# Sixteen heads at a time: the maximum and subtraction of attention in one piece, score banks released together

## What is computed

```python
Q = _apply_rope(jnp.einsum('bsd,ed->bse', x, wq), cos, sin)
K = _apply_rope(jnp.einsum('bsd,ed->bse', x, wk), cos, sin)
V = jnp.einsum('bsd,ed->bse', x, wv)
# 16 heads of 16
scores = jnp.einsum('bhqd,bhkd->bhqk', Q, K) / math.sqrt(DIM_K)
weights = jax.nn.softmax(scores, axis=-1)
out = jnp.einsum('bhqk,bhkd->bhqd', weights, V)
```

## Time and profile before

| | us |
|---|---|
| median of three runs | 1210.27 |
| profiled execution | 1208.59 |
| span of the instructions in that execution | 1206.8 |
| PE busy, all stages | 977.0 (81%) |
| DVE busy | 692.0 (57%) |
| POOL busy | 650.4 (54%) |
| ACT busy | 524.6 (43%) |
| first scores matmul of attention | starts at 126.06 |
| last weighted values | start at 273.55 |

### The profile page before, as it was taken

How to read it: one execution, slowest core, us unless ns; L and a number is a source line. 1 busy time by engine, 2 the same in 40 slices (tenths; PEclk the granted TensorE clock), 3 DMA queues, 4 the chain that set the end, 5 groups by cost and what they waited for, 6 DMA issues and landing times. The chain is left out here.

```text
span 1206.8 us, 22495 instructions
## 1 busy us (share of the span) xinstructions
PE 977.0 (81%) x6878; PEld 869.3 (72%) x6878; DVE 692.0 (57%) x1539; ACT 524.6 (43%) x1080; POOL 650.4 (54%) x588
## 2 busy tenths in 40 slices
PE   6269699997569999398888699995169999999970
PEld 5258377776568898266666499995169999999970
DVE  1435599985666767569999346642723333333335
ACT  0011377772222222334433456563056676666650
POOL 0115578764544444223334489873057777777750
PEclk9689899997679999778888799996579999999995
DMA  7651345540000000000000510004346666666656
GB/s 255 194 219 49 85 153 160 167 139 18 0 1 1 0 0 0 0 1 0 0 0 0 212 75 14 14 27 166 139 147 203 197 194 198 193 202 190 205 177 225
DMA packets 61189, 127.32 MB, mean 106 GB/s; under 512 B 11929, under 2 KB 25954, under 8 KB 59794
## 3 DMA queue, kind: packets, MB, share of 16 engines
q1 hardware_dynamic: 52146, 103.81, 26.6%
q0 software_dynamic: 4848, 14.72, 3.5%
q10 hardware_dynamic: 4144, 8.16, 1.9%
HBM read 104.57 MB, written 24.31 MB: 107 GB/s over the span
## 5 line engine op out<-in xcount | busy, mean ns | idle before, releaser
L121 DVE CAST place<-place 128x512 fp32r<-128x512 f32 (+6 forms) x263 | 134.6, 544 | 212.9 <-PE moe_down L127 78.5
L2015 POOL TENSOR_TENSOR place<-place,place 128x512 fp32r<-128x512 f32 x84 | 138.0, 1643 | 51.5 <-DVE place L121 45.4
L2041 PE MATMUL moe_up<-place,place 128*128 128x128 f32 x1376 | 161.8, 276 | 0.0
L2041 PEld LDWEIGHTS moe_up<-place,place 128*128 128x128 f32 x1376 | 158.3, 193 | 0.0
L127 PE MATMUL moe_down<-place,place 128*128 128x256 f32 x1008 | 131.1, 286 | 0.4 <-POOL place L2015 0.4
L127 PEld LDWEIGHTS moe_down<-place,place 128*128 128x128 f32 x1008 | 123.4, 191 | 0.6 <-issue 0.6
L2113 ACT ACTIVATE place<-moe_up,place 128x128 f32<-128x128 f32 x344 | 97.5, 366 | 13.4 <-POOL place L2015 13.1
L2100 ACT ACTIVATE place<-place 128x2048 f32 x44 | 84.0, 1912 | 43.6 <-PEq L1837 29.9
L1168 POOL TENSOR_TENSOR place<-place,place 128x384 fp32r<-128x384 f32 x57 | 58.4, 1024 | 78.0 <-DVE place L121 78.0
L127 PE MATMUL up<-place,place 128*128 128x384 f32 x342 | 72.6, 350 | 19.8 <-POOL place L1162 19.8
L1148 ACT ACTIVATE place<-up,place 128x384 f32<-128x384 f32 x57 | 33.2, 582 | 114.6 <-PE up L127 114.6
(11 more groups left out here) (241 smaller groups left out, 2051.6 us busy)
## 6 DMA issues: line engine op xcount, KB each, us to landing
place<-w_remainder SPq DMA_DIRECT2D x172, 256.0 KB
place<-in_w_dram SPq DMA_DIRECT2D x4, 4096.0 KB, 13.5
place<-in_w_dram SPq DMA_DIRECT2D x16, 512.0 KB, 3.8
w_remainder<-place SPq DMA_DIRECT2D x16, 512.0 KB, 2.9
place<-value_rows SPq DMA_DIRECT2D x64, 64.0 KB, 2.4
place<-choices ACTq DMA_DIRECT2D x5, 768.0 KB, 8.7
place<-in_patches_dram SPq DMA_DIRECT2D x9, 384.0 KB, 4.4
place<-in_e_dram SPq DMA_DIRECT2D x2, 1152.0 KB, 7.4
```

What stands on the lines that cost most here:

```text
L121: return eng.tensor_copy(out, x)
L2015: pool.tensor_tensor(lo[f], raw[f], hi[f].bitcast(F32), ALU.subtract).then_inc(h_split, 1)
L2041: last = pe.matmul(p1[u][k // HK][:, (k % HK) * P:(k % HK + 1) * P], ws[u][:, c, k * P:(k + 1) * P], xT[u][:, c, :], start=(c == 0), stop= ...
```

## The change

The two score tensors of two banks become one tensor of four banks. `soften` makes one reduction over 69x1104 and one subtraction over 69x1104 in place of two of each over 69x552; it waits for the scores of both halves first, and it raises `s_read` once for a batch. `scores(n)` waits once, ahead of its first half, for `s_read` to reach n, that is for the whole batch before; the `keyed` wait and the `s_mm` increment stay one for each half. `exp(n)` waits for `s_read` n + 1 in place of 2n + 2, which is the same point.

```diff
@@ -710,14 +710,14 @@
         self.w2_rest = self.dram("w2_remainder", [P, E * KF, D])
 
         with ExitStack() as ctx:
-            sc = [ctx.enter_context(nc.psum_tensor(f"scores{c}", [P, 2, 512], F32)) for c in range(C)]
+            sc = ctx.enter_context(nc.psum_tensor("scores", [P, 4, 512], F32))
             tp = [ctx.enter_context(nc.psum_tensor(f"turned_probs{j}", [P, 512], F32)) for j in range(2)]
             ov = ctx.enter_context(nc.psum_tensor("out_values", [P, 512], F32))
             ot = ctx.enter_context(nc.psum_tensor("out_turned", [P, 512], F32))
             block = ctx.enter_context(nc.Block())
             ov_heads = ov[0:S, 0:HEADS * VW].rearrange("p (h w) -> p h w", w=VW)
             ot_view = ot[:, 0:C * S].rearrange("p (c s) -> p c s", s=S)
-            half = [sc[c][0:S, :, 0:H2 * S].rearrange("p g (j s) -> p g j s", s=S) for c in range(C)]
+            sc_heads = sc[0:S, :, 0:H2 * S].rearrange("p g (j s) -> p g j s", s=S)
 
             @block.sync
             def _(sp):
@@ -779,10 +779,10 @@
                 def scores(n):
                     for c in range(C):
                         pe.wait_ge(keyed, n * C + c + 1)
-                        if n >= 1:
-                            pe.wait_ge(s_read, (n - 1) * C + c + 1)
+                        if n >= 1 and c == 0:
+                            pe.wait_ge(s_read, n)
                         for r in range(2):
-                            last = pe.matmul(sc[c][0:S, r, 0:HALF * S], self.qF[:, c, n * S:(n + 1) * S],
+                            last = pe.matmul(sc[0:S, 2 * c + r, 0:HALF * S], self.qF[:, c, n * S:(n + 1) * S],
                                              k2[n % KB][:, c, r, :, :].rearrange("p a s -> p (a s)"), start=True, stop=True)
                         last.then_inc(s_mm, 1)
 
@@ -840,14 +840,12 @@
                 link = Steps(dve, step, 0)
 
                 def soften(n):
-                    for c in range(C):
-                        at = slice(c * 2 * H2, (c + 1) * 2 * H2)
-                        dve.wait_ge(s_mm, n * C + c + 1)
-                        link(dve.tensor_reduce(top[0:S, at].rearrange("p (g j) -> p g j", j=H2), half[c], AX_X, ALU.max))
-                        if n >= 2 and c == 0:
-                            dve.wait_ge(exp_done, n - 1)
-                        dve.tensor_tensor(prob[n % 2][0:S, at].rearrange("p (g j) s -> p g j s", j=H2), half[c],
-                                          inner(top[0:S, at].rearrange("p (g j) -> p g j", j=H2), S), ALU.subtract).then_inc(s_read, 1)
+                    dve.wait_ge(s_mm, n * C + C)
+                    link(dve.tensor_reduce(top[0:S].rearrange("p (g j) -> p g j", j=H2), sc_heads, AX_X, ALU.max))
+                    if n >= 2:
+                        dve.wait_ge(exp_done, n - 1)
+                    dve.tensor_tensor(prob[n % 2][0:S].rearrange("p (g j) s -> p g j s", j=H2), sc_heads,
+                                      inner(top[0:S].rearrange("p (g j) -> p g j", j=H2), S), ALU.subtract).then_inc(s_read, 1)
 
                 def spread_few(n):
                     if n >= 2:
@@ -886,7 +884,7 @@
             @block.scalar
             def _(act):
                 def exp(n):
-                    act.wait_ge(s_read, n * C + C)
+                    act.wait_ge(s_read, n + 1)
                     if n >= 2:
                         act.wait_ge(pt_mm[0], n - 1)
                         act.wait_ge(pt_mm[1], n - 1)
```

## The result

Beside runs of the kernel before (median 1212.85 us of 20), five runs of the changed kernel have a median of 1234.95 us: a ratio of 1.0191, interval 1.0168 to 1.0214. The first comparison gave 1234.96 against 1210.69 (1.0197, 1.0169 to 1.0224). The change makes the kernel 22 to 24 us slower: 22.1 by the medians of the first pair, 24.3 by those of the second. 1231 was forecast.

A forecast was written before the change was run, and what follows sets the result against it. PE was taken as full and DVE nearly so. Batches of 4.88 us replacing 4.20 gave +19.0 over 28 steps, plus 1.6 at attention's start and 0.2 at its end: 20.8, hence 1231 us, range 1226 to 1247.

The forecast's parts named there:

- Softmax of a batch: DVE's merged reduction, semaphore step and merged subtraction: 2.64 us a batch in place of 2.90.
- Start: DVE's first reduction, waiting for both score halves, begins 2.12 us after the loads, 0.93 later than before.
- Release: From the end of DVE's whole subtraction to PE's next score loads: 0.12 us.
- Ring: Scores, softmax and release in closed sequence: 4.88 us a batch replacing 4.20, +19.0 us over 28 steps; chance 0.71.
- The alternation of the loads: Score loads 4.01 and 4.38 us apart in turn were to become equal, 4.9 apart, without PE's wait for ACT's copy.
- The wait of PE for DVE's subtraction: New PE idle time before each batch's scores, about 0.9 us a batch, near 25 us in total.
- PE was to be busy 82% of a step: PE in attention: busy 4.0 of 4.88 us a batch, where it had been full.
- Start of the stage: First batches of attention at a low clock: loads of batch 3 move from 145.24 to 146.8, +1.6 us.
- End of the stage: After the last scores' loads, softmax ends later but ACT's queue is ahead: +0.2 us, between 0 and 0.7.
- `finish` and `spread_few` take ... about 1 us: DVE's work behind each softmax, from 246.08 to 247.03, was to stay hidden after the change.
- the faster one: Rival: DVE's saving decides, PE stays full at 4.01 us a batch, 1205 us in all; chance 0.04.
- The falling clock: Rival: PE's idleness in attention drops its clock for 28% of the time, +16 us, 1247; chance 0.20.

The follow-up runs named there:

- extra_inside_one: One VectorE fill of 128x200 added between maximum and subtraction of the changed kernel; median 1259.9 us, ratio 1.0403 against the kernel before.
- start_whole: Kernel before, with VectorE waiting for the scores of both halves before its first reduction, four instructions kept; median 1236.9 us, ratio 1.0169 against the kernel before.
- extra_inside: Two VectorE fills of 128x200 added between maximum and subtraction of the changed kernel; median 1279.1 us, ratio 1.0545 against the kernel before.

## Why the prediction was right, and where it was off

**Softmax of a batch.** 1.29 + 0.05 + 1.30 was forecast; 1.304, 0.03 and 1.303 were measured, 2.63 in all for 2.64. **Start.** 2.12 and 2.12. **Release.** 0.12 and 0.12. **Ring.** 4.88 forecast, 4.875 measured, so +18.95 for the 28 steps against +19.0. The alternation of the loads and the wait for ACT's copies are gone; the clock is 1.00 from 150 to 260 us. The wait of PE for DVE's subtraction was to total near 25 us, 0.9 a batch, and comes to 24.2, but that agreement is luck: it is 0.69 a batch, and 4.26 us of the total stand before the scores of batch 2. PE was to be busy 82% of a step and is 86%: its records fill 4.18 us a batch, not 4.0. The step of the loads does not depend on it. **Start of the stage.** The loads of batch 3 are at 147.31 and not at 145.24: +2.1, of which 0.3 is an offset that the stage starts with (first loads at 126.39 against 126.06); 1.6 was forecast. **End of the stage.** From the last scores' loads to the output projection 15.3 us and 15.8 before: -0.5 for +0.2, since ACT and the rest of the queue were ahead. Sum for the stage: 20.5 measured, 20.8 forecast; the two small terms missed by +0.5 and -0.7 and nearly cancel.

The forecast of 1231 is 4 below the measurement, and attention, which was right within 0.3 us, is not where it went wrong. Two other things are left. The base, "That execution is 1.7 below the median of the runs shown; against the median the sum gives 1231.1", rested on three runs at 1210.3; on the three chips of the later runs the medians of the kernel before were 1213.9, 1213.3 and 1212.9, and 20.8 on the last would have been 1233.7. And the sum has no term for the stages after attention. They vary by some 7 us from execution to execution, and the medians of before and after lie 1.7 to 3.8 us further apart than attention explains. In the first comparison (1210.69 and 1234.96) nearly all of the miss is of this second kind. Its cause is open.

One row was read too lightly. "`finish` and `spread_few` take ... about 1 us" took L858's 0.41 as its price, although L858 had taken 0.56 to 0.57 in every second batch. After the change it takes 1.24 to 1.27 there. That it still costs nothing is the slack of the ring: DVE still waits 0.42 us before its reduction in those batches (203.06) and 1.28 in the others. The conclusion stood, with less to spare than I had written; and in the other batches it stood by luck, since L856 began 0.24 us ahead of GpSimd's L760. Behind it, as in extra_inside_one, it would have taken about 2.5 us, more than its 0.41 and the 1.28 of slack together.

Of the rivals, the faster one fell with the measured 1.30 us an instruction; it needed 0.86. DVE did get the saving that one large tile brings, 2.63 us for 2.90, and it bought nothing, because PE was the full engine and DVE's part of it had been hidden. The falling clock did not come, but was near, as shown above.

## What to carry to other kernels

Merging two half-size instructions saves a fixed cost on one engine, but where the halves carry a handover both ways (begin on the first half, give the first half back), it turns a pipeline into a ring whose stations add up; add them up first: fill, both instructions, release, against the step of now. Keeping either end split was enough here to save most of it (+0.3% and +0.6% in place of +1.9%). And before an instruction with two SBUF inputs is called short, look at what GpSimd does at that time: here L858's place in time, not its size, set its length.

## What the hardware showed that was not expected

L858, a VectorE product of two SBUF operands over 80x256, took 0.41 to 0.42 us when no GpSimd instruction was running as it began, and up to 2.6 in start_whole and in both runs with fills inside the ring. In the fourteen traces it took longer than 0.42 us 205 times, and each time it ended 0.28 to 0.29 us after the GpSimd instruction that was running when it began. A GpSimd instruction that began later did not hold it up, such as L760 at 206.48 above. VectorE's instructions that read PSUM were not touched: L846 and L849 keep 0.72 to 0.73 us and L866 0.42 under the same GpSimd instructions. The Trainium skill, page "GPSIMD Engine Reference", section "8. Key points", says that GpSimd shares its SBUF interfaces with VectorE and contends with its instructions that have two SBUF inputs; the rows agree, and show that the wait lasts to the end of GpSimd's instruction, which takes 2.36 us in the last example.

The clock's response was steep. In the changed kernel PE was idle for 0.69 us before each batch's scores, and the clock stayed at 1.00. With 0.33 us more in the ring PE was idle for 1.02 us there in most batches, 1.78 where L858 had been held up, and the mean clock was 0.94; with 0.67 more, for mostly 1.35 or 1.78 us, it was 0.81. In extra_inside a batch at the low level took 7.15 us in place of 5.54. How much of the fall is due to the fill and how much to the longer idle time behind a held L858 was not separated: of the five batches of extra_inside_one with slow scores four came behind 1.66 to 1.78 us of idleness, one behind 1.02, and other batches behind 1.78 kept the full clock. The Trainium skill's page "TensorE: Matmul & The Clock Gate", section "A second HAM failure mode: psum-queue depth-cycling", tells of a matmul kernel that idles briefly again and again and falls back and forth between the two clock levels: the changed kernel does not show that oscillation, the two with a longer ring do.
